# Loading the first attention's first two stacks from inside the preparation

## The reference, cut to what matters

```python
x = x + L0_xattn(layernorm(x), ctx, ctx)      # 16 heads of 16, softmax(q k^T / sqrt(256)) v
x = x + L0_ffn(layernorm(x), ...)             # 64 experts, top 8
x = x + L1_xattn(layernorm(x), ctx, ...)      # causal, with projections
x = x + L1_ffn(layernorm(x), ...)             # 16 blocks, top 4
```

## Time and profile before

| | us |
|---|---|
| median of 3 runs (lowest, highest) | 1137.54 (1134.96, 1138.79) |
| the profiled execution's own time | 1142.81 |
| its span, first to last instruction | 1140.9 |
| last write of the preparation issued | 49.92 |
| first instructions of attention 0 | 53.35 |
| its first query-row scores, step 0 | 59.80 |
| query-row scores of step 1 | 68.03 |
| its first key-row scores, step 0 | 74.12 |

### The profile page before, as it was taken

The page is one execution under the profiler, slowest core; times in us unless marked ns, Lnnn a source line. Parts: engine busy times, 40 slices in busy tenths (PEclk is TensorE's granted clock), DMA queues, the critical chain, the costliest instruction groups (busy, mean ns, idle before and its releaser), DMA issues. The chain is left out here.

```text
span 1140.9 us, 21554 instructions
## 1 busy us (share of the span) xinstructions
PE 941.4 (83%) x5670; PEld 635.6 (56%) x5670; DVE 616.9 (54%) x1818; ACT 361.7 (32%) x884; POOL 535.8 (47%) x514
## 2 busy tenths in 40 slices
PE   1178788869199999999999999606788896799999
PEld 1135445447167777777777777404666674465665
DVE  6568998777144444444444444385887761333220
ACT  3526555443122222222222222111454563112211
POOL 4400676766567777777777777350524100111010
PEclk9999977798699999999999999855899997699999
DMA  6564443104466566656666776246777432000000
GB/s 217 173 163 134 98 95 89 40 25 134 134 200 208 184 215 193 216 176 197 218 213 218 220 218 197 88 198 199 210 203 200 110 82 91 0 14 5 19 19 19
DMA packets 78863, 160.69 MB, mean 141 GB/s; under 512 B 18448, under 2 KB 44048, under 8 KB 76480
## 3 DMA queue, kind: packets, MB, share of 16 engines
q1 hardware_dynamic: 59264, 112.23, 33.3%
q0 software_dynamic: 19520, 47.41, 13.3%
HBM read 118.09 MB, written 41.22 MB: 140 GB/s over the span
## 5 line engine op out<-in xcount | busy, mean ns | idle before, releaser
L1306 PE MATMUL ex_ps<-ex_w_gu,ex_rows_t 128*128 x640 | 260.7, 489 | 0.5 <-ACT ex_rows_t L1373 0.5
L1273 POOL DMA_INDIRECT expert_outs<-ex_result,slot_places x160 | 157.4, 984 | 69.0 <-DVE ex_result L1419 58.0
L1268 POOL DMA_INDIRECT ex_rows<-moe_rows,slot_tokens x160 | 153.9, 962 | 54.2 <-issue 48.8
L886 POOL DMA_INDIRECT expert_lists<-rt_number,rt_idx x128 | 124.2, 970 | 110.4 <-DVE rt_idx L993 67.8
L1325 PE MATMUL ex_ps<-ex_w_down,ex_hidden_t 96*128 x640 | 166.6, 382 | 1.0 <-DVE ex_hidden_t L1411 1.0
L621 ACT ACTIVATE a_probs<-a_ps 128x512 f32<-128x512 f32 (+1 forms) x256 | 133.3, 540 | 103.4 <-PE a_ps L483 53.7
L466 PE MATMUL a_ps<-stacked_keys,a_qst 96*128 96x256 bf16 (+1 forms) x512 | 113.2, 295 | 55.0 <-DMA stacked_keys<-k_stack 24.0
L1379 ACT ACTIVATE ex_act_g<-ex_ps 128x192 f32<-128x192 f32 x160 | 52.8, 330 | 320.2 <-PE ex_ps L1306 320.2
L1419 DVE TENSOR_SCALAR ex_result<-ex_ps,ex_rows 128x256 f32<-128x256 f32 x160 | 77.4, 484 | 93.6 <-PE ex_ps L1325 93.6
L1306 PEld LDWEIGHTS ex_ps<-ex_w_gu,ex_rows_t 128*128 128x128 f32 x640 | 109.8, 192 | 9.9 <-issue 1.8
L1325 PEld LDWEIGHTS ex_ps<-ex_w_down,ex_hidden_t 96*128 96x128 f32 x640 | 108.1, 188 | 12.2 <-issue 2.3
(11 more groups left out here) (221 smaller groups left out, 1417.9 us busy)
## 6 DMA issues: line engine op xcount, KB each, us to landing
ex_w_gu<-in_w_gu_dram SPq DMA_DIRECT2D x64, 384.0 KB, 3.5
gathered<-expert_outs SPq DMA_DIRECT2D x16, 1024.0 KB, 5.7
ex_w_down<-in_w_down_dram SPq DMA_DIRECT2D x64, 192.0 KB, 4.0
a_qst<-q_stack SPq DMA_DIRECT2D x32, 192.0 KB, 3.9
stacked_keys<-k_stack SPq DMA_DIRECT2D x32, 192.0 KB, 3.9
a_qst<-q_stack SPq DMA_DIRECT2D x32, 128.0 KB, 3.7
stacked_keys<-k_stack SPq DMA_DIRECT2D x32, 128.0 KB, 3.7
k_stack<-split_parts SPq DMA_DIRECT2D x8, 384.0 KB, 2.6
```

The source lines that it names most:

```text
L886: nc.gpsimd.indirect_dma_start(k.lists, bass.IndirectOffsetOnAxis(ap=self.idx[:, t, s:s + 1], axis=0), self.number[:, t, s:s + 1], None).t ...
L1268: nc.gpsimd.indirect_dma_start(rows[:, t % R, :], None, k.xn.rearrange("t p d -> (t p) d"), bass.IndirectOffsetOnAxis(ap=k.ids[:, begin + ...
L1273: nc.gpsimd.indirect_dma_start(k.outs, bass.IndirectOffsetOnAxis(ap=k.places[:, begin + t:begin + t + 1], axis=0), result[:, t % R], None) ...
L1306: last = pe.matmul(ps[:, 2 + j % 2, 0:2 * FF], rows_t[:, j % 2, c * P:(c + 1) * P], w_gu[:, bass.ds(ring, 1), c, :].rearrange("p a n -> p ...
```

## The change

`qst` of attention 0 and `split_parts` are allocated around the preparation and attention 0, and so are the four semaphores of the stack loads and the two of the writes. In the preparation, after the writes of batch 2, SP waits for `written[0]` to reach 32 and issues the twelve stack loads of steps 0 and 1; then it writes batches 3 to 7. It no longer waits for the writes at the end. Attention 0 leaves out these twelve loads; ahead of each later batch's stack loads SP waits for the writes of that batch's parity up to that batch. Attention 1 keeps its own `qst` and its order.

```diff
--- before.py
+++ after.py
@@ -131,6 +131,9 @@
             sp.wait_ge(loaded, 16 * len(pairs))
 
 
+KINDS = 2
+
+
 def prepare(nc, k):
 
 
@@ -146,7 +149,7 @@
         eps = sb("ln0_eps", [P, 1], F32)
         xn = sb("ln0_out", [P, 2, 2, D], F32)
         rest = sb("split_rest", [P, 2, 2, DC * SEQ], F32)
-        parts = sb("split_parts", [P, 2, 2, 3, DC * SEQ], BF16)
+        parts, written = k.split_parts, k.stacks_written
         ps = ctx.enter_context(nc.psum_tensor("ps_prep", [P, 8, 512], F32))
         x_in = [sem(f"x_in{b}") for b in range(BATCH)]
         c_in = [sem(f"ctx_in{b}") for b in range(BATCH)]
@@ -161,8 +164,6 @@
         rested = sem("rested")
         middle = sem("middle")
         split = sem("split")
-        written = [sem("written0"), sem("written1")]
-        KINDS = 2
 
 
         K0, Q0 = 0, 1
@@ -193,12 +194,12 @@
                 for b in range(BATCH):
                     load_x(b)
                     load_ctx(b)
-                for b in range(BATCH - 2):
+                for b in range(BATCH):
                     write(b, b % 2)
-                for u in range(2):
-                    write(BATCH - 2 + u, u)
-                for u in range(2):
-                    sp.wait_ge(written[u], 16 * KINDS * (BATCH // 2))
+                    if b == 2:
+                        sp.wait_ge(written[0], 16 * KINDS)
+                        for part in range(2):
+                            load_stacks(sp, k.q0_stack, k.k0_stack, k.qst0, k.kst, k.stack0_in, 0, part)
 
             @block.vector
             def _(dve):
@@ -316,6 +317,19 @@
         sweep(nc, used)
 
 
+def load_stacks(sp, q_stack, k_stack, qst, kst, stack_in, b, u):
+
+    half = HSTEP * SEQ
+    part = u % 2
+    for stack, tile in ((q_stack, qst), (k_stack, kst)):
+        rows = stack[bass.ds(b, 1)].rearrange("b t (d h) n -> d (b t) (h n)", d=DH)[:, :, part * half:(part + 1) * half]
+        at = 0
+        for run, n in enumerate(RUNS):
+            src = rows[:, run:run + 1].to_broadcast([DH, n, half]) if tile is qst else rows[:, 0:n]
+            sp.dma_start(tile[at:at + n * DH, u].rearrange("p s n -> p (s n)"), src).then_inc(stack_in[u], 16)
+            at += n * DH
+
+
 def attention(nc, k, name, q_stack, k_stack, values, scale, causal, out, side):
 
 
@@ -335,7 +349,7 @@
         used = []
         sem = phase_semaphores(nc, ctx, name, used)
         kst = k.kst
-        qst = sb("qst", [ROWS + MROWS, 4, HSTEP, SEQ], BF16)
+        qst = sb("qst", [ROWS + MROWS, 4, HSTEP, SEQ], BF16) if causal else k.qst0
         v_raw = sb("v_raw", [P, 2, 2, D], F32)
         v_aug = sb("v_aug", [P, 2, 2, HEADS, VW], F32)
         probs = sb("probs", [P, HSTEP, 4 * P], F32)
@@ -354,7 +368,8 @@
         max_t = ps[0:2 * HSTEP, 6, SEQ:SEQ + P].bitcast(BF16)
         outs_qd = ps[:, 7, :].rearrange("p (j n) -> p j n", j=2)
 
-        stack_in = [sem(f"stack_in{j}") for j in range(4)]
+        stack_in = [sem(f"stack_in{j}") for j in range(4)] if causal else k.stack0_in
+        used.extend([] if causal else k.stack0_in + k.stacks_written)
         v_in = [sem("v_in0"), sem("v_in1")]
         max_in = [sem(f"max_in{j}") for j in range(4)]
         v_ready = sem("v_ready")
@@ -408,20 +423,15 @@
 
             @block.sync
             def _(sp):
-                half = HSTEP * SEQ
-
                 def load(st):
                     i, u = st
                     b, part = batch_of(st), u % 2
                     if part == 0:
                         side.before_load(sp, i, u // 2)
-                    for stack, tile in ((q_stack, qst), (k_stack, kst)):
-                        rows = stack[bass.ds(b, 1)].rearrange("b t (d h) n -> d (b t) (h n)", d=DH)[:, :, part * half:(part + 1) * half]
-                        at = 0
-                        for run, n in enumerate(RUNS):
-                            src = rows[:, run:run + 1].to_broadcast([DH, n, half]) if tile is qst else rows[:, 0:n]
-                            sp.dma_start(tile[at:at + n * DH, u].rearrange("p s n -> p (s n)"), src).then_inc(stack_in[u], 16)
-                            at += n * DH
+                    if causal or not (isinstance(i, int) and i == 0 and u < 2):
+                        if not causal and part == 0:
+                            sp.wait_ge(k.stacks_written[u // 2], 16 * KINDS * (i + 1))
+                        load_stacks(sp, q_stack, k_stack, qst, kst, stack_in, b, u)
                     if part == 0:
 
                         wait(sp, v_ready, b - 1)
@@ -1978,8 +1988,13 @@
 
         k.indirect = lambda n: ctx.enter_context(nc.semaphore(f"indirect_{n}"))
         constants(nc, k, ctx)
-        prepare(nc, k)
-        attention(nc, k, "a0", k.q0_stack, k.k0_stack, dram["ctx"], 1.0 / float(np.sqrt(np.float32(D))), False, k.ao, Route())
+        with ExitStack() as first:
+            k.qst0 = first.enter_context(nc.sbuf_tensor("a0_qst", [ROWS + MROWS, 4, HSTEP, SEQ], BF16))
+            k.split_parts = first.enter_context(nc.sbuf_tensor("split_parts", [P, 2, 2, 3, DC * SEQ], BF16))
+            k.stack0_in = [first.enter_context(nc.semaphore(f"a0_stack_in{j}")) for j in range(4)]
+            k.stacks_written = [first.enter_context(nc.semaphore(f"stacks_written{u}")) for u in range(2)]
+            prepare(nc, k)
+            attention(nc, k, "a0", k.q0_stack, k.k0_stack, dram["ctx"], 1.0 / float(np.sqrt(np.float32(D))), False, k.ao, Route())
         with ExitStack() as late:
             k.gathered = late.enter_context(nc.sbuf_tensor("gathered", [P, 2, 2, TOP_K, D], F32))
             k.rows_in = [late.enter_context(nc.semaphore(f"combine_rows_in{u}")) for u in range(2)]
```

## The result

The changed kernel is faster: ratio 0.9935 to the kernel before, 95% interval 0.9913 to 0.9957, that is 7.4 us (4.9 to 9.9) of 1137.5; medians 1127.97 against 1137.9 over 20 runs each. Forecast were 9.4 us and 1128.1. The profiled execution took 1136.89, around a span of 1134.9.

The account below looks back on a forecast made before the run. A chain of DMA waits up to the first key-row scores at 74.12, with DVE and PE standing still, was taken as the bound; -2.3 - 6.4 - 2.9 + 1.8 + 0.4 = -9.4 us gave 1128.1 us, range 1123 to 1134.

Parts of the forecast that it names:

- Wait: End of the preparation: SP no longer waits for the last writes to land, saving 2.3 us.
- step 0's stack: Start of attention 0: PE can start with the stage instead of waiting for these loads, saving 6.4 us.
- step 1's stack: Attention 0, between steps 0 and 1: DVE goes on without idling for PE's scores, saving 2.9 us.
- key-row path: Attention 0, up to the first key-row scores: maxima copies queue behind step 2's stack and values, costing 0.4 us (bounds 0, 1.2).
- The preparation's stall: Batch 3's writes land late behind the twelve loads, delaying ACT's copies of batch 5 and DVE: 1.8 us (0.9 to 4).
- 0.1 to 0.4 for the receipt: Preparation: time from batch 3's data ending at 39.8 to its landing, put near 39.9.
- upper case: Preparation: batch 4's writes mix in with batch 3's, making the landing 3 to 4 us late.
- The bound of 1.2 us for the values: Attention 0: upper bound on the maxima copies' delay, the time of 0.26 MB of values at 198 GB/s.
- A: Preparation: loads and writes mix, it stalls 4 us, gain 6.4 us, 1131 us; chance 0.14.
- B: Attention 0: PE reaches its fast clock before step 2, gaining perhaps 1.5 us more, 1126.5 us; chance 0.09.
- C: Later stages: more low-clock stretches, 4.1 us each, eat the gain; slower, 1140 to 1145 us; chance 0.04.
- D: Preparation's end moves by all that attention 0 gains, writes landing 9 us later still; 1137 us; chance 0.03.

Follow-up runs that it names:

- e1_nowait: Kernel before with only the wait for the last writes at the preparation's end removed, stack loads still in attention 0; ratio to before 0.9987.
- e1_split: Changed kernel with step 0's loads after batch 1's writes and step 1's after batch 3's; ratio to before 0.9858, repeated 0.989.
- e2_tiny: Changed kernel with twelve loads of 1/32 the bytes in place, real loads back in attention 0; preparation ended at 51.5 us, executed once, no ratio.
- e1_split_next: As e1_split, with step 2's stack and values also issued ahead of the seven constants' loads; ratio to before 0.9863.

## Why the prediction was right

The mechanism was right: each wait went as worked out, and the stall came at the place, with the waiter and for the cause that were named. One term was mis-sized, the stall, and the landmarks gained 8.5 us where 9.4 were forecast. That the median fell on the forecast 1128.1 is in part luck: the medians are 9.9 us apart, the ratios say 7.4 and 11.3.

- **Wait, step 0's stack, step 1's stack** (2.3, 6.4, 2.9 us): each as forecast. e1_nowait shows the first alone; the PE and DVE rows above show that the other two waits are gone. The meeting of engines took 0.7 us (52.97 to 53.70), forecast 0.8. e1_split, where nothing is paid back in the preparation, has them net of the key-row path: 11.1 us, forecast 11.6 - 0.4 = 11.2.
- **The preparation's stall** was named with its place, waiter and cause, but mis-sized: 2.9 us, forecast 1.8, within its bounds (0.9 to 4). Windows of the changed kernel (columns as in rows 5):

```profile
37.00:37.50 0.50, 0.00 (x0) 0.00 (x0) 0.47 (x2) 0.00 (x0) 0.35 (x1) 1.00 0.64 133
37.50:38.00 0.50, 0.00 (x0) 0.00 (x0) 0.43 (x3) 0.00 (x0) 0.00 (x0) 1.00 1.03 232
38.00:38.50 0.50, 0.00 (x0) 0.00 (x0) 0.50 (x2) 0.00 (x0) 0.00 (x0) 1.00 1.06 367
...
41.50:42.00 0.50, 0.00 (x0) 0.00 (x0) 0.50 (x2) 0.32 (x1) 0.00 (x0) 1.00 0.70 244
```

  The dip at 37.0 to 37.5 is the end of the loads, forecast 37.5; from then to 42.0 the four writes run, and by the bytes of the windows the first two are through near 39.8 (an estimate that takes them first), as forecast; on the clock of the kernel before all of this is 0.2 us later. The step that failed is "with 0.1 to 0.4 for the receipt", of which 0.1 was used: the second write was landed only at 40.7, 0.9 us after its data. No row and no run shows 0.1 to 0.4. The kernel before shows 0.5, for batch 2's second write, which was issued at 28.02 and landed 2.6 us later, at 30.6:

```profile
29.80:30.00 0.20, 0.20 (x3) 0.20 (x2) 0.20 (x1) 0.18 (x1) 0.00 (x0) 1.00 1.01 353
30.00:30.20 0.20, 0.20 (x3) 0.05 (x1) 0.20 (x1) 0.20 (x1) 0.00 (x0) 1.00 0.56 185
30.20:30.60 0.40, 0.26 (x2) 0.00 (x0) 0.40 (x2) 0.40 (x2) 0.08 (x1) 1.00 0.00 0
```

  Its data ends at 30.1. By the same working e2_tiny, with the same four writes and idle rings, has 0.5 too (data to 39.1, landed at 39.6). So 0.4 us of the miss could have been read before, another 0.2 is that offset of the two traces, and the last 0.4 appears only behind the loads' bytes: whether it is a longer receipt or batch 4's bytes mixing in, which the forecast had as its upper case, no run here separates. The same lines show that batch 2's write was through at 30.1 and not at 29.6, as the forecast had it. The loads' end came right only because they also took about 7.4 us (30.0 to 37.4, an estimate) instead of 7.9, which is luck. And the forecast's lower bound of 0.9 us was too low: issue alone gave 1.7 (e2_tiny).
- **The key-row path**: 65.65 - 53.73 = 11.9 us, forecast 11.8. The stack, forecast up to 0.1 us late, kept PE waiting for 0.8 us and the maxima rows for 0.8. The bound of 1.2 us for the values should read 1.3 (0.26 MB at 198 GB/s), which changes nothing else.
- **Attention 0 after that** was taken as unchanged. In the profiled pair 2.5 us of the 8.5 were gone at the end (1140.9 to 1134.9); the stretch was 4.4 us longer. The second trace of before, 7.7 us shorter than the first, shows that one pair can't carry such a difference. The timed ratios, 7.4 and 11.3 us, lie on both sides of 8.5.
- **Rivals.** A, more stall, is where the size went: 8.5 us is a third of the way from the forecast's 9.4 to A's 6.4. B, an earlier fast PE, did not come in the changed kernel: in its three traces the first fast key-row matmul starts 12.2, 10.2 and 8.7 us after the first of all, in the two of before 9.9 and 8.4. In both traces of the split it starts after 4.4 and 4.3 us, which no run explains. In e1_split_next it starts after 8.8 us and the stretch is only 0.6 to 0.8 us longer, so B seems worth less than 1 us (an estimate from these traces). C, more low clock, is real as scatter, but not as a loss that the timed runs show. D fell: the preparation's end moved by 2.9 us.

## What to carry to other kernels

A load hoisted into a stage takes its place in the queue of the stage's writes, in issue time and in bytes: find which engine waits for the next writes and how much slack it has (here 1.8 us against 7.5 us of loads), and cut the hoisted work into pieces that fit between two batches, or give that engine one buffer more; either gave back the whole stall. A single profile of this kernel says nothing on differences under 9 us in its end time (two of the kernel before ended 8.7 us apart), while its landmarks up to a stage's start repeat within 0.2 us: compare changes by the landmarks next to the edit, and the total by many runs.

## What had not been expected

- Half the issues with all the bytes stalled the preparation more (3.8 us) than the twelve issues did (2.9): the writes waited for the loads' last byte, and the six loads ended later than the twelve. Freeing SP early gained nothing (9.0 us from issue to landing).
- Back-to-back issues take SP longer: the four writes behind the loads took 0.42, 0.49, 0.67 and 1.09 us each, where a lone one takes 0.36.
- In the first trace of the changed kernel PE's slow level lasted through 11 us of nearly full work (11.35 of 12.0 us busy from 65 to 77, granted clock column 1.00). "TensorE: Matmul & The Clock Gate" of the Trainium skill (section "What's actually happening") has the slow level as the default that activity releases. The traces agree that the fast level comes under load, but when it comes differs from trace to trace of one kernel by up to 3.5 us (8.7 to 12.2), though its instructions up to there are the same.
